# Attention on one core: odd groups of the mixing go to the other partition halves and a second PSUM bank, and the outputs share the two banks

## The reference, cut to what matters

```
q, k, v = xs @ Wq.T, xs @ Wk.T, 2 * (xs @ Wv.T)        # 8 heads of 16 channels per position
q, k, v_h = l2norm(q), l2norm(k), l2norm(v)
attn_head = softmax(einsum('bnhd,bngd->bnhg', v_h, v_h))  # mixes the 8 heads of one position
q, k = attn_head mixed into q, k
attn = softmax(einsum('bnhd,bnhe->bnde', k, q))        # 16 x 16 for each position
out = einsum('bnhd,bnde->bnhe', v, attn)
out = transpose(out, (0, 3, 1, 2)).reshape(b, n, 128) @ proj_w.T + proj_b
```

## Time and profile before

| | us |
|---|---|
| median of 3 runs | 3333.34 |
| the profiled execution | 3327.52 |
| its span in the trace | 3325.7 |
| TensorE busy | 2987.1 (90%) |
| VectorE, ScalarE, GpSimd busy | 1866.8, 1275.8, 570.3 |
| mean granted clock of TensorE over the span | 0.955 |

### The profile page before, as it was taken

One profiled execution on the slowest core, in us unless ns is written; L12 is line 12 of the kernel. 1 busy time (PEld: TensorE's weight loads), 2 busy tenths in 40 slices (PEclk: granted clock), 3 DMA queues, 4 the chain that ended last, 5 costly groups with the idle time before them and its releaser, 6 DMA issues. The chain is left out here.

```text
span 3325.7 us, 143922 instructions
## 1 busy us (share of the span) xinstructions
PE 2987.1 (90%) x62769; PEld 2207.7 (66%) x62769; DVE 1866.8 (56%) x3334; ACT 1275.8 (38%) x2841; POOL 570.3 (17%) x419
## 2 busy tenths in 40 slices
PE   6686989999999999999998995889888898988897
PEld 5463369766666666666665443777777777777777
DVE  4452542566666666666665773555555555555553
ACT  3453552422222222222222443444444444444431
POOL 0000030022222222222221222111111111111111
PEclk8787889999999999999999996999999999999999
DMA  6877000021112121212114985555555555564551
GB/s 143 229 227 198 1 1 1 13 47 45 46 44 46 43 46 43 46 44 45 45 44 174 414 326 139 84 85 95 103 109 85 104 91 113 85 110 85 104 85 49
DMA packets 1015824, 318.88 MB, mean 96 GB/s; under 512 B 863345, under 2 KB 1002158, under 8 KB 1010350
## 3 DMA queue, kind: packets, MB, share of 16 engines
q1 hardware_dynamic: 692626, 169.81, 24.7%
q10 hardware_dynamic: 322844, 143.73, 15.8%
HBM read 157.66 MB, written 155.75 MB: 94 GB/s over the span
## 5 line engine op out<-in xcount | busy, mean ns | idle before, releaser
L845 DVE TENSOR_TENSOR terms<-spec,ps_z 112x456 f32<-112x456 f32 x1024 | 575.0, 623 | 404.4 <-PE ps_z L728 404.4
L738 PEld LDWEIGHTS ps_q<-inv_w,prod 112*57 112x57 f32 x16384 | 450.9, 133 | 174.6 <-issue 172.2
L738 PE MATMUL ps_q<-inv_w,prod 112*57 112x56 f32 x16384 | 484.4, 217 | 1.2 <-DVE prod L851 1.2
L826 POOL TENSOR_TENSOR prod<-terms 112x456 f32<-112x456 f32 x256 | 297.6, 1162 | 1000.6 <-DVE terms L845 1000.6
L728 PE MATMUL ps_z<-x_half,fwd_w 120*112 120x456 f32 x1024 | 458.4, 570 | 0.0
L783 ACT ACTIVATE q_half<-ps_q 121x448 f32<-121x448 f32 x255 | 138.9, 545 | 827.3 <-PE ps_y L746 827.3
L1131 POOL TENSOR_TENSOR k_blocks<-k_mixed,same_of 128x896 f32<-128x896 f32 x112 | 193.4, 1727 | 1071.2 <-ACT k_mixed L1274 1071.2
L1180 PE MATMUL ps_l<-q_mixed,k_blocks 32*64 32x64 f32 x12544 | 230.1, 220 | 66.4 <-issue 65.6
L1180 PEld LDWEIGHTS ps_l<-q_mixed,k_blocks 32*64 32x64 f32 x12544 | 205.3, 133 | 83.2 <-issue 75.2
L1157 PEld LDWEIGHTS ps_s<-v_blocks 128*64 128x64 f32 x6272 | 199.0, 141 | 90.0 <-issue 81.0
L728 PEld LDWEIGHTS ps_z<-x_half,fwd_w 120*112 120x112 f32 x1024 | 160.4, 176 | 121.9 <-issue 106.1
(11 more groups left out here) (140 smaller groups left out, 4340.0 us busy)
## 6 DMA issues: line engine op xcount, KB each, us to landing
qk_heads<-st_qk ACTq DMA_DIRECT2D x56, 476.0 KB, 4.6
qk_rows<-qk_heads SPq DMA_DIRECT2D x56, 476.0 KB, 6.8
conv_in<-v_sb ACTq DMA_DIRECT2D x112, 224.0 KB, 3.3
v_in<-conv_in SPq DMA_DIRECT2D x512, 49.0 KB
conv_out<-y_sb ACTq DMA_DIRECT2D x512, 49.0 KB
y<-conv_out SPq DMA_DIRECT2D x8, 1792.0 KB, 13.6
x_in<-in_x SPq DMA_DIRECT2D x8, 1568.0 KB, 9.5
shortcut<-short ACTq DMA_DIRECT2D x8, 1568.0 KB, 6.2
```

The lines of the kernel that those rows point to most:

```text
L738: last = pe.matmul(ps_q[64 * ri:64 * ri + NF, c * SIDE:(c + 1) * SIDE], prod[b % 2][:, x, c * NF:(c + 1) * NF], k.inv_w[:, x, ri * SIDE:(r ...
L826: pool.tensor_tensor(prod[b % 2][:, 1, :], terms[b % 2][:, 2, :], terms[b % 2][:, 3, :], ALU.add).then_inc(prod_i_r, 1)
L845: last = dve.tensor_tensor(terms[b % 2][:, x, :], k.spec[0:NFFT, s, bass.ds(c * CC, CC), :].rearrange("p c f -> p (c f)"), ps_z[b % 2][z][ ...
```

## The change

`ps_m` and `ps_o` are put together into one tensor of two banks, `ps_mo`. The mixing of group g goes to bank g % 2, at columns 272 to 502. For an odd g the upper half of the rows goes to the lower half of the partitions and the other way round. The outputs go to columns 0 to 271 of bank 0. They take v in the order that fits the swapped halves, so that their results land where they did before. Since the two now share bank 0, `mix(i)` waits until `leave(i-3)` has read the outputs, and `outputs(i-2)` waits until `leave_mix(i)` and `weigh(i)` have read the mixing of the same round. The order within a round becomes mix, scores, outputs, logits on TensorE, `leave_mix` ahead of `exp_s` on ScalarE, and `weigh` ahead of `mask` and `leave` on VectorE. The number of instructions stays.

```diff
--- before.py
+++ after.py
@@ -1029,6 +1029,8 @@
 
 
 
+
+
     TB, BPB, GB, GU = 112, 4, 28, 14
     NB = BATCH * TOK // (TB * BPB)
     NU = 2 * NB
@@ -1037,6 +1039,8 @@
     NIN = 4
     RPI = TOK // 16
     RH = RPI // 2
+    MC = (GU + 3) * HD
+    MW = GU // 2 * QKM
     with ExitStack() as ctx:
         def sb(n, shape):
             return ctx.enter_context(nc.sbuf_tensor(n, shape, F32))
@@ -1066,7 +1070,8 @@
         oT = [sb(f"oT{m}", [128, HD, RPI]) for m in range(2)]
         x1 = sb("x1_in", [128, TOK])
         res = [sb(f"res{m}", [RH, 4, CH]) for m in range(4)]
-        ps_a, ps_m, ps_o, ps_f = (psum(n) for n in ("ps_qkv", "ps_mix", "ps_o", "ps_qkv_fin"))
+        ps_a, ps_f = (psum(n) for n in ("ps_qkv", "ps_qkv_fin"))
+        ps_mo = psum("ps_mix_o", (128, 2, 512))
         ps_s, ps_l = psum("ps_s", (128, 2, 512)), psum("ps_l", (128, 2, 512))
         xn_loaded = [sem(f"xn_loaded{m}") for m in range(3)]
         st_stored = [sem(f"st_stored{m}") for m in range(2)]
@@ -1163,10 +1168,13 @@
                 if i:
                     pe.wait_ge(q_r, i)
                     pe.wait_ge(km_r, i)
+                if i >= 3:
+                    pe.wait_ge(o_r, i - 2)
                 for g, gb in groups(i):
                     for a in range(2):
                         rows = slice(64 * a, 64 * a + 64)
-                        last = pe.matmul(ps_m[rows, g * QKM:g * QKM + 64], eb[i % 2][rows, g, :], strided(qk[n % NIN][rows], gb * QKW, [[1, 64]]), start=True, stop=True)
+                        half, at = 64 * (a ^ g % 2), MC + g // 2 * QKM
+                        last = pe.matmul(ps_mo[half:half + 64, g % 2, at:min(at + 64, 512)], eb[i % 2][rows, g, :], strided(qk[n % NIN][rows], gb * QKW, [[1, min(64, 512 - at)]]), start=True, stop=True)
                 last.then_inc(m_ps, 1)
 
             def logits(i):
@@ -1186,9 +1194,14 @@
                 pe.wait_ge(p_r, i + 1)
                 if i:
                     pe.wait_ge(o_r, i)
+                if unit(i + 2):
+                    pe.wait_ge(q_r, i + 3)
+                    pe.wait_ge(km_r, i + 3)
                 for g, gb in groups(i):
                     for a in range(2):
-                        last = pe.matmul(ps_o[64 * a:64 * a + 64, g * HD:g * HD + 64], vb[n % NIN][:, gb, a, :], pn[i % 2][:, a, g:g + 4, :], start=True, stop=True)
+                        r = a ^ g % 2
+                        last = pe.matmul(ps_mo[64 * r:64 * r + 64, 0, g * HD:g * HD + 64], vb[n % NIN][:, gb, r, :], pn[i % 2][:, a, g:g + 4, :],
+                                         start=True, stop=True)
                 last.then_inc(o_ps, 1)
 
             def final(b, u):
@@ -1211,12 +1224,12 @@
             scores(0)
             for i in range(ROUNDS):
                 bk = AHEAD * BPB + 2 * i
+                if unit(i):
+                    mix(i)
                 if unit(i + 1):
                     scores(i + 1)
                 if unit(i - 2):
                     outputs(i - 2)
-                if unit(i):
-                    mix(i)
                 if unit(i - 1):
                     logits(i - 1)
                 if i in FINS:
@@ -1265,13 +1278,13 @@
                 act.activation(pe_[i % 2][:].rearrange("p r g e -> p r (g e)"), ps_l[:, :, 0:GU * HD], ACT.Exp).then_inc(l_exp, 1)
 
             def leave_mix(i):
-                ps = ps_m[:, 0:GU * QKM].rearrange("p (g x) -> p g x", x=QKM)
+                ps = ps_mo[:, :, MC:MC + MW].rearrange("p j (g x) -> p g j x", x=QKM)
                 act.wait_ge(m_ps, i + 1)
                 if i >= 2:
                     act.wait_ge(q_r, i - 1)
                     act.wait_ge(k_r, i - 1)
-                act.activation(dsq[i % 2][:], ps[:, :, HD:HD + 1], ACT.Square).then_inc(d_r, 1)
-                act.activation(km[i % 2][:], ps[:, :, HD + 1:], ACT.Copy).then_inc(km_r, 1)
+                act.activation(dsq[i % 2][:].rearrange("p (g j) x -> p g j x", j=2), ps[:, :, :, HD:HD + 1], ACT.Square).then_inc(d_r, 1)
+                act.activation(km[i % 2][:].rearrange("p (g j) x -> p g j x", j=2), ps[:, :, :, HD + 1:], ACT.Copy).then_inc(km_r, 1)
 
             def store(b, u):
                 act.wait_ge(f_r, b * 8 + u + 1)
@@ -1294,12 +1307,12 @@
                 bk = AHEAD * BPB + 2 * i
                 if i % 2 == 0 and i // 2 + AHEAD - 1 < NB:
                     root(i // 2 + AHEAD - 1)
+                if unit(i):
+                    leave_mix(i)
                 if unit(i + 1):
                     exp_s(i + 1)
                 if i % 2 == 1 and i // 2 + AHEAD - 1 < NB:
                     store_heads(i // 2 + AHEAD - 1)
-                if unit(i):
-                    leave_mix(i)
                 if unit(i - 1):
                     exp_l(i - 1)
                 if bk < NB * BPB:
@@ -1343,14 +1356,15 @@
 
             def weigh(i):
                 a = i % 2
-                ps = ps_m[:, 0:GU * QKM].rearrange("p (g x) -> p g x", x=QKM)
+                ps = ps_mo[:, :, MC:MC + MW].rearrange("p j (g x) -> p g j x", x=QKM)
                 dve.wait_ge(d_r, i + 1)
                 dve.reciprocal(wgt[a][:], dsq[a][:]).then_inc(w_r, 1)
                 dve.wait_ge(w_r, i + 1)
                 dve.wait_ge(km_r, i + 1)
                 if i >= 2:
                     dve.wait_ge(l_ps, i - 1)
-                dve.tensor_tensor(qm[a][:, 0:GU, :], ps[:, :, 0:HD], wgt[a][:].to_broadcast([128, GU, HD]), ALU.mult).then_inc(q_r, 1)
+                dve.tensor_tensor(qm[a][:, 0:GU, :].rearrange("p (g j) d -> p g j d", j=2), ps[:, :, :, 0:HD],
+                                  wgt[a][:].rearrange("p (g j) x -> p g j x", j=2).to_broadcast([128, GU // 2, 2, HD]), ALU.mult).then_inc(q_r, 1)
 
             def divide(i):
                 a = i % 2
@@ -1369,7 +1383,7 @@
                 if i % UPI == 0 and b >= 2:
                     dve.wait_ge(f_ps, 8 * (b - 1))
                 n, g0 = i // 2, i % 2 * GU
-                dve.tensor_tensor(oT[b % 2][:, :, r0:r0 + GU].rearrange("p e g -> p g e"), ps_o[:, 0:GU * HD].rearrange("p (g e) -> p g e", e=HD),
+                dve.tensor_tensor(oT[b % 2][:, :, r0:r0 + GU].rearrange("p e g -> p g e"), ps_mo[:, 0, 0:GU * HD].rearrange("p (g e) -> p g e", e=HD),
                                   qk[n % NIN][:, g0:g0 + GU, QKM:QKM + 1].to_broadcast([128, GU, HD]), ALU.mult).then_inc(o_r, 1)
 
             def add_bias(b, u):
@@ -1391,12 +1405,12 @@
                         normalize(pr // 2 - 1)
             mask(0)
             for i in range(ROUNDS):
+                if unit(i):
+                    weigh(i)
                 if unit(i + 1):
                     mask(i + 1)
                 if unit(i - 2):
                     leave(i - 2)
-                if unit(i):
-                    weigh(i)
                 if unit(i - 1):
                     divide(i - 1)
                 if i in FINS:
```

## The result

| | before | after |
|---|---|---|
| median of 4 runs each, same chip | 3334.73 us | 3530.15 us (3527.16 to 3530.72) |
| ratio, 95% interval | | 1.0579 [1.0558, 1.06] |
| span of the profiled execution | 3325.7 us | 3525.4 us |
| mean granted clock of TensorE | 0.955 | 0.943 |

The change makes the kernel 5.8% slower. The forecast was 3447 us with a range to 3525: right in the direction, 83 us too low, and 5 us outside of the range. The span of the profiled execution grew by 199.7 us.

A forecast was written before the change was run, and what follows sets the result against it. TensorE was taken as the bound, busy 2987.1 of 3325.7 us. The terms 109 - 30 + 30 + 5 = +114 us on 3327.5 gave 3441.5, and 5.8 more for the median 3447, with an 8 in 10 range of 3350 to 3525.

The forecast's parts named there:

- Part 1: TensorE's mixing over four quadrants: from some 1.78 us to 0.95, saving 0.83 us a unit, 93 us over 112 units.
- Part 2: TensorE's outputs wait for weigh and leave_mix: stops of 2.8 and 1.06 us in turn; with the mixing's saving, +109 us.
- Part 3: TensorE's "issue" idle time in the logits: the stops give back about half of 62.9 us, -30, bounds 0 and -63.
- Part 4: TensorE's clock: the 2.8 us stop, 53 times, brings the lower level, a third taken, +30 us of 0 to +90.
- Part 5: Small edits: outputs in swapped column order +5 us; mix's wait, exponentials, strided reads and GpSimd's earlier input 0.
- The other zeros: mix(i) waiting for leave(i-3), the exponentials of the scores, the strided reads of two banks: each put at 0 us.
- the fourth: TensorE's clock takes most: each long stop brings a stretch at half clock, 3507 us; chance 0.13.
- The second: No change: TensorE is paced by its code, all 89 us of "issue" vanish in the waits, around 3333 us; chance 0.07.
- The first: The outputs' wait ends under the scores, the mixing's saving comes through whole, 3240 us; chance 0.07.
- The third: Packing doesn't happen: the mixing stays at 1.78 us, the outputs' starts don't move, 3452 us; chance 0.10.

The follow-up runs named there:

- the first experiment: Two kernels against the kernel before: new order and all new waits without four-quadrant mixing, 3563.04 us; the same without the outputs' wait, 3346.99 us.
- the best order: Changed kernel with squares, clamp, normalize behind weigh, root behind leave_mix, k_blocks waiting for clamp or normalize: 3340.48 us; with the mixing as before, 3351.44 us.
- the filler: Changed kernel plus two 512-column matmuls, result unread, between scores and outputs in odd rounds: 3505.31 us, 1.052 against the kernel before.

## Why the prediction was wrong in size

**Part 1 held.** Forecast 0.95 us from start to start, measured 0.957 (median), and the sum over the attention -86 us for -93. The trace has 56 matmuls whose quadrants share both row halves in 1.03 us, not 1.85. The Trainium skill's rule on weight loads that spoke against this part ("TensorE: Matmul & The Clock Gate", Part 3) is at odds with it.

**Part 2 held in its sum, by two errors that cancel.** Forecast was a stop of some 205 us, measured are 208.5 (7.0 before). The order of releasers came out as written. But the odd rounds' outputs come at a median of T + 6.04, not 5.4, mostly since `normalize` takes longer beside GpSimd (T + 5.50 with GpSimd held back). And the scores end at T + 3.1 on average, not 2.64, with the gaps in the mixing and the scores. That shortens the stop by about as much. Parts 1 and 2 together: 201.5 - 86 = +116 us for the +109 forecast.

**Part 3 is the step that failed.** I let the stops give back half of the logits' "issue" time, -30 us, and of the denser mixing I wrote that it "can add some" and left it at no number. The logits' "issue" time rose by 31, and the gaps in all bursts from 116 to 143. The kernels of the first experiment take this apart, with one trace each: the new order brings the gaps from 116 to 131 us, the wait from there to 105, and the packing from there to 143. So the stops did give back 26, about as forecast. The term put at nothing failed: the packed mixing uses up as much code in half of the time and added 38, and the order added 15. The pair of kernels in the best order shows the same by itself: there the packing alone adds 52 us of gaps. The upper bound of 0 was the mistake, and with it the top of the range.

**Part 4 had the mechanism and less than half of the size.** I took a third of the 53 long stops and +30 us. There were 36 half-clock stretches more, 136 us or at most 68 us of work, and the filler shows that some 25 us of it reach the end. The 1.00 of the earlier trace rows, on which I leaned, is of a kernel that stands idle for over 2 us only 7 times in these 400 us. The changed one does so 21 times.

**Part 5 failed at "GpSimd gets its input earlier, and nobody waits for it: 0".** Nobody waits for it, but some of VectorE's instructions are held up while it runs, just in the list that the stop hangs on: 38 us. The outputs with swapped halves mostly take 1.78 us at full clock from start to start, where before has 1.73. The swap isn't the reason: the kernel with only the order and the waits has 1.78 too, and the packed one in the best order 1.73. So the +5 for the swap was nothing. The other zeros weren't tested one by one.

The terms as measured, 116 + 31 + 68, make 215, where the span grew by 200. So at least some 15 us of the half-clock time cost nothing, by subtraction; no run shows where. Against the forecast, part 3 is off by 61 us and part 4 by 38. GpSimd's 38 are inside part 2, where the late end of the scores covers them.

Of the rivals, the fourth (3507) was nearest in number and right in part. The second, a kernel paced by its code, was wrong as forecast, since the "issue" time doesn't vanish in the stops; its idea takes most of the packing's gain once the stop is gone. The first would have needed `normalize` elsewhere in the list, and with it moved the time came to 3340, not 3240. The third is refuted by the burst.

## What to carry to other kernels

A wait in front of a burst costs what stands before its releaser in the releaser's own list: here 216 us, and next to nothing once that list was reordered (1.0045 with the wait, 1.003 without). A burst made shorter with the same number of instructions is worth less than its time when TensorE already shows "issue" gaps; compare the gain with a kernel that leaves the instructions out. When an engine's work moves in time, look at which other engine then runs beside it, even where nobody waits for it.

## What the runs showed of the hardware

- A 112x32 copy on VectorE went from 133 to 646 and 1040 ns on average beside a GpSimd product of 1.68 us, a clamp of 0.21 us took 1.23, and the two shown in the timelines ended within 0.06 us of the product's end.
- TensorE's "issue" gaps rose and fell with instructions per time: 116 us before, 193 packed in the best order, 139 with half of its mixing instructions but all of its matmul time, 82 with a projection between the bursts. One packet of the instruction queue stood for 255 or 256 records, the gaps of over 0.3 us lay at whole multiples of that, and nearly all ended 1.2 to 1.8 us after a packet's landing. Why some of them come later than others stays open.
- 64 by 64 tiles over all four quadrants ran at 17 ns a matmul (0.957 us from start to start, for 56), though neighbours share their row halves.
- The lower clock mostly came behind idle times of 2 to 3 us, but not behind each: TensorE was idle for over 2 us 78 times after the change and 22 times before, and had 49 and 13 stretches at half clock. They lasted 184 us with the stop and 82 when two matmuls whose result nobody reads filled a part of it.
